# Cross attention on one core: GpSimd's work laid out turn by turn

## What is computed

```python
q = (x @ Wq + bq).reshape(b, ql, H, D_Q)          # b=16, ql=100, H=16, D_Q=64
k = (ctx @ Wk + bk).reshape(b, kl, H, D_Q)        # kl=1444
v = (ctx @ Wv + bv).reshape(b, kl, H, D_Q)
scores = einsum('bqhd,bkhd->bhqk', q, k) / sqrt(D_Q)
attn = softmax(scores, axis=-1)
out = einsum('bhqk,bkhd->bqhd', attn, v).reshape(b, ql, H * D_Q) @ Wo + bo
y = layernorm(x + out) * gamma + beta
```

## Time and profile before

| | us |
|---|---|
| median of 3 runs | 888.61 (886.81 to 889.89) |
| the profiled execution | 888.62, span 886.8 |
| TensorE busy | 860.3 (97%) |
| VectorE busy | 832.9 (94%) |
| ScalarE busy | 732.0 (83%) |
| GpSimd busy | 483.2 (54%) |

### The profile page before, as it was taken

How to read it: one execution, slowest core, us unless ns; L and a number is a source line. 1 busy time by engine, 2 the same in 40 slices (tenths; PEclk the granted TensorE clock), 3 DMA queues, 4 the chain that set the end, 5 groups by cost and what they waited for, 6 DMA issues and landing times.

```text
span 886.8 us, 19588 instructions
## 1 busy us (share of the span) xinstructions
PE 860.3 (97%) x7328; PEld 618.4 (70%) x7328; DVE 832.9 (94%) x1053; ACT 732.0 (83%) x989; POOL 483.2 (54%) x516
## 2 busy tenths in 40 slices
PE   8799999899999999999999999999999999999996
PEld 7476766577677677776777776766777777767675
DVE  4899899999999999999999999999999999998984
ACT  3687868888888888898988887888888988888983
POOL 2142497975637385465727555373854657276210
PEclk7999999999999999999999999999999999999999
DMA  9598988999999999999999999999999999999995
GB/s 238 130 165 192 192 164 171 209 206 191 227 194 225 216 218 218 220 216 219 213 206 231 211 197 222 196 219 227 214 217 214 216 221 217 194 205 209 210 180 125
DMA packets 683041, 180.79 MB, mean 204 GB/s; under 512 B 654596, under 2 KB 682052, under 8 KB 682948
## 3 DMA queue, kind: packets, MB, share of 16 engines
q1 hardware_dynamic: 681332, 178.48, 102.3%
q10 hardware_dynamic: 1344, 0.53, 0.2%
q0 software_dynamic: 272, 0.53, 0.2%
HBM read 15.35 MB, written 0.82 MB: 18 GB/s over the span
## 4 chain that ended last, share of the span: by engine, by line
DVE 43%; PE 38%; issue 8%; ACT 5%; DMA 5%; SPq 2%; ACTq 0%; DVEq 0%; POOLq 0%; POOL 0%
DVE p_lo L921 20%; PE ps L642 17%; DVE nmax L906 16%; PE ps L603 16%; DMA pt_hi<-p_hi 4%; ACT p L1030 2%; PE ps L458 2%; ACT p_hi L1038 2%; DVE rsum L912 2%; PE ps L450 1%; DVE rinv L914 1%; DVE c_max L808 1%; PE ps L465 1%; DMA bq_pairs<-in_L_xattn_bq_dram 1%; SPq L402 1%
## 5 line engine op out<-in xcount | busy, mean ns | idle before, releaser
L921 DVE SCALAR_TENSOR_TENSOR p_lo<-p,rinv,p_hi 128x1444 f16<-128x1444 f32 x200 | 367.9, 1840 | 2.4 <-ACT p_hi L1038 2.0
L1038 ACT ACTIVATE p_hi<-p,rinv 128x1444 f16<-128x1444 f32 x200 | 299.7, 1499 | 57.3 <-DVE rinv L914 53.4
L906 DVE TENSOR_REDUCE nmax<-ps 128x1 f32<-128x1446 f32 x200 | 330.0, 1650 | 6.0 <-PE ps L603 6.0
L1030 ACT ACTIVATE p<-ps,nmax 128x1446 f32<-128x1446 f32 x200 | 292.7, 1464 | 48.6 <-DVE nmax L906 45.7
L642 PE MATMUL ps<-pt_hi,c_hi 128*128 128x256 f16 (+1 forms) x1232 | 253.6, 261 | 5.4 <-DMA pt_hi<-p_hi 3.8
L642 PE MATMUL ps<-pt_hi,c_lo 128*128 128x256 f16 (+1 forms) x1232 | 253.4, 261 | 0.0
L603 PE MATMUL ps<-ct_hi,g_hi 128*128 128x482 f16 (+3 forms) x624 | 155.9, 368 | 0.7 <-ACT p L1030 0.6
L603 PE MATMUL ps<-ct_hi,g_lo 128*128 128x482 f16 (+3 forms) x624 | 156.2, 368 | 0.0
L603 PE MATMUL ps<-ct_lo,g_hi 128*128 128x482 f16 (+3 forms) x624 | 156.2, 368 | 0.0
L642 PEld LDWEIGHTS ps<-pt_hi,c_hi 128*128 128x128 f16 x1232 | 114.4, 98 | 43.0 <-issue 10.4
L1137 POOL CAST g_hi<-g_raw 128x400 f16<-128x400 f32 x60 | 32.5, 542 | 203.7 <-DVE g_raw L831 203.7
(11 more groups left out here) (128 smaller groups left out, 820.2 us busy)
## 6 DMA issues: line engine op xcount, KB each, us to landing
c_raw<-in_ctx_dram SPq DMA_DIRECT2D x32, 256.0 KB
pt_hi<-p_hi SPq DMA_TRANSPOSE x200, 3.5
pt_lo<-p_lo SPq DMA_TRANSPOSE x200, 3.6
c_raw<-in_ctx_dram SPq DMA_DIRECT2D x16, 192.0 KB
c_raw<-in_ctx_dram SPq DMA_DIRECT2D x48, 18.0 KB
out_dram<-late_sb SPq DMA_DIRECT2D x16, 50.0 KB
x_sb<-in_x_dram SPq DMA_DIRECT2D x1, 600.0 KB
o_t<-in_L_xattn_Wq_dram SPq DMA_DIRECT2D x2, 256.0 KB, 4.5
```

The lines of the kernel that those rows point to most:

```text
L906: dve.tensor_reduce(nmax[:, n % RING:n % RING + 1], ps[:, bank:bank + 3, 0:KEYW], AX.XY, ALU.max, negate=True).then_inc(s_nm, 1)
L921: dve.scalar_tensor_tensor(out=p_lo[:, n % LOS, 0:KL], in0=p32[:, n % P32S, 0:KL], scalar=rinv[:, i:i + 1], in1=p_hi[:, par, 0:KL], op0=AL ...
L1030: act.activation(p32[:, n % P32S, :].rearrange("p (k w) -> p k w", w=KEYW), ps[:, bank:bank + 3, 0:KEYW], ACT.Exp, bias=nmax[:, i:i + 1], ...
L1038: act.activation(p_hi[:, par, 0:KL], p32[:, n % P32S, 0:KL], ACT.Copy, scale=rinv[:, i:i + 1]).then_inc(s_hi, 1)
```

## The change

GpSimd's program becomes one loop over turns. At the head of turn n it waits until VectorE has written the low part of tile n-1 (s_lo). Then come the pieces of that turn: the scales of the next queries and a result split at r = 0, a result split at r = 1, a query split at each of r = 2 to 5, a context piece at each of r = 6, 8 and 9 (CLO_AT), the last result split at r = 7, the tail copies, the inverse deviation and the first result split of the current batch at r = 10, finish_rows at r = 11. The once-only pieces get turns of their own: the matrices' low parts n = 13 to 16, the addition to x n = 18, x's low parts n = 19 to 22, M's low parts n = 24 to 27. These use a scratch tile of their own, left_scaled. SyncE's transpose ct_lo moves to r = 10 in every window.

```diff
-    CT_LO_AT = 8
-    CT_LO_AT_FIRST = 9
+    CT_LO_AT = 10
+    CLO_AT = (6, 8, 9)
...
+        left_scaled = sb("left_scaled", [P, HG * P])
...
-                if r == (CT_LO_AT if w else CT_LO_AT_FIRST) and w + 1 < B:
+                if r == CT_LO_AT and w + 1 < B:
                     transpose_context_lo(w + 1)
...
-            def context_lo(b):
-                par = b % 2
+            def context_lo(b, g):
+                par, tiles = b % 2, slice(TG * g, TG * g + TG)
                 pool.wait_ge(s_al, b + 1)
...
-            for w in range(B):
-                b = w + 1
...
+            def once(n):
+                g = n - A16_AT - 1
+                if 0 <= g < NG:
+                    pool.wait_ge(s_16h, g + 1)
+                    heads = slice(HG * g, HG * g + HG)
+                    leave_lo(g, a_sb[:, heads, :], a16[:, heads], ax_scale[:, 0:1])
+                if n == X16_AT:
...
+                    pool.tensor_tensor(x_sb[:, :, :], x_sb[:, :, :], rows_b[0:QL, 0:1, :].to_broadcast([QL, B, D]),
+                                       ALU.add).then_inc(s_xres, 1)
+                g = n - X16_AT - 1
+                if 0 <= g < NX:
...
+                g = n - M16_AT - 1
+                if 0 <= g < NG:
+                    leave_m_lo(g)
+
+            for n in range(N):
+                w, r = window(n)
+                b, g_at = w + 1, (G_AT if w else G_AT_FIRST) + 1
+                if n > 0:
+                    pool.wait_ge(s_lo, n)
+                if b < B and r == (0 if w else g_at - 1):
+                    query_scales(b)
+                if in_parts(w - 1) and r < 2:
+                    if w == 2 and r == 0:
+                        pool.wait_ge(s_16, NG + NX)
+                        split_results(w - 1, 0)
+                    split_results(w - 1, r + 1)
+                if b < B and g_at <= r < g_at + NG:
+                    split_queries(b, r - g_at)
+                once(n)
+                if b < B and r in CLO_AT:
+                    context_lo(b, CLO_AT.index(r))
+                if in_parts(w - 1) and r == 7:
                     split_results(w - 1, NG - 1)
                     output_scale(w - 1)
...
+                if r == 10:
+                    if b < B:
+                        pool.wait_ge(s_cl, NT * b)
+                        context_tail(b)
+                    if w > 0:
+                        inverse_deviation(w - 1)
+                    if w > 1 and in_parts(w):
+                        split_results(w, 0)
+                if r == 11 and w > 0:
                     finish_rows(pool, w - 1)
             inverse_deviation(B - 1)
```

More of the change, by code:

```diff
@@ L1158, in leave_m_lo @@
             def leave_m_lo(g):
-                heads, at = slice(HG * g, HG * g + HG), c_scaled[:, :].rearrange("p (n w) -> p n w", w=P)
+                heads, at = slice(HG * g, HG * g + HG), left_scaled[:, :].rearrange("p (n w) -> p n w", w=P)
                 pool.wait_ge(s_mh, g + 1)
@@ L1162, in leave_m_lo @@
                     pool.wait_ge(s_ml, g)
+                else:
+                    pool.wait_ge(s_16, NG + NX)
                 pool.tensor_scalar(at, m_sb[:, heads, :], m_scale[:, :], 1.0, ALU.mult, ALU.mult).then_inc(s_mw, 1)
@@ L1173, in context_tail @@
                 pool.tensor_copy(c_tail[0:2 * KTAIL, par, :], c_hi[0:2 * KTAIL, par, KT - 1, :]).then_inc(s_chl, 1)
-            def context_lo(b):
-                par = b % 2
+            def context_lo(b, g):
+                par, tiles = b % 2, slice(TG * g, TG * g + TG)
                 pool.wait_ge(s_al, b + 1)
[L1178 to L1189, removed]
+                if NT * b + g > NT:
+                    pool.wait_ge(s_cl, NT * (b - 1) + g)
+                pool.tensor_scalar(c_scaled[:, :], c_raw[:, par, tiles, :].rearrange("p t d -> p (t d)"),
+                                   alpha[:, par:par + 1], 1.0, ALU.mult, ALU.mult).then_inc(s_cs, 1)
+                pool.wait_ge(s_cs, NT * (b - 1) + g + 1)
+                pool.wait_ge(s_chi, NT * b + g + 1)
+                pool.tensor_tensor(c_lo[:, par, tiles, :].rearrange("p t d -> p (t d)"), c_scaled[:, :],
+                                   c_hi[:, par, tiles, :].rearrange("p t d -> p (t d)"), ALU.subtract).then_inc(s_cl, 1)
             def inverse_deviation(b):
@@ L1199, in leave_lo @@
                 n, w = raw.shape[1], raw.shape[2]
-                at = c_scaled[:, 0:n * w].rearrange("p (n w) -> p n w", w=w)
+                at = left_scaled[:, 0:n * w].rearrange("p (n w) -> p n w", w=w)
                 if i:
@@ L1217, in _ @@
                              bv_sb[:, :].unsqueeze(2).to_broadcast([P, PAIRS, P])).then_inc(s_bvw, 1)
-            for w in range(B):
-                b = w + 1
-                if b < B:
-                    query_scales(b)
[L1223 to L1234, removed]
+            def once(n):
[5 more added lines that the diff above has]
+                if n == X16_AT:
+                    emptied(pool, J_R)
+                    emptied(pool, J_X3)
+                    pool.wait_ge(s_ax, 2 * NG)
+                    pool.tensor_tensor(x_sb[:, :, :], x_sb[:, :, :], rows_b[0:QL, 0:1, :].to_broadcast([QL, B, D]),
+                                       ALU.add).then_inc(s_xres, 1)
+                g = n - X16_AT - 1
+                if 0 <= g < NX:
+                    pool.wait_ge(s_16h, NG + g + 1)
+                    batches = slice(XG * g, XG * g + XG)
+                    leave_lo(NG + g, xT[:, batches, :], x16[:, batches], ax_scale[:, 1:2])
+                g = n - M16_AT - 1
+                if 0 <= g < NG:
+                    leave_m_lo(g)
@@ L1235, in _ @@
                     split_results(w - 1, NG - 1)
                     output_scale(w - 1)
[L1237 to L1255, removed]
@@ L1256, in _ @@
-                if w > 0:
-                    inverse_deviation(w - 1)
+                if r == 10:
[7 more added lines that the diff above has]
+                if r == 11 and w > 0:
                     finish_rows(pool, w - 1)
```

## The result

| | us |
|---|---|
| before, median | 889.25 (886.81 to 890.25, 4 runs) |
| changed kernel, median | 927.98 (925.42 to 932.22, 4 runs) |
| ratio after/before | 1.0439, 95% interval 1.0415 to 1.0463 |
| profiled execution, span | 930.3 |

What follows compares the result with a forecast made beforehand. TensorE was taken to bound the kernel. Onto 888.6 us came even-window stalls 24.9, window 0 1.8, odd windows 0.7 and clock 7, less 3 at the start: 920.0 us, range 905 to 932.

Steps and rivals of the forecast that it cites:

- The deciding term: Late ct_lo transpose stalls TensorE in the shared tile's scores, ends of windows 2 to 14: 7 x 3.55 = 24.9 us.
- VectorE's lag: From the end of a tile's scores to VectorE's start on them; taken as 0.35 us in each even-window stall.
- Odd windows: With 13 tiles, ct_lo lands just in time: 0 to 0.4 us each, taken as 0.1, seven times: 0.7 us.
- Window 0: ct_lo moves from r = 9 to 10 and lands late: between 0 and 2.6 us, taken as 1.8.
- The clock: TensorE's granted clock falls to 0.50 behind stalls: 1.4 us in five of seven, 7 us, bounds 0 and 12.
- The start: TensorE's early waits for first output rows and M's low parts shrink: gain 0 to 5.2 us, taken as 3.
- VectorE's low part: Line 921, held up by GpSimd in the kernel before; its mean should fall from 1.84 to 1.74 us or less.
- The overrun at r = 10: GpSimd's pieces exceed the gap between low parts: nothing to 0.95 us, taken as 0.5 us a window.
- the relief: VectorE's low parts freed from GpSimd: per two windows 1.8 us given back of 2.4, worth zero on the path.
- context_scale's new wait of 0.4 us: At r = 10 VectorE's context_scale waits for tail copies started that turn: nothing to two casts of 0.52 us.
- TensorE bounds, with VectorE 2% behind: Over 25 turns, tiles 87 to 112, TensorE is busy 102.86 of 102.86 us and VectorE has 1.8 us free.

Runs made afterwards that it cites:

- the filler experiment: Changed kernel with 17 extra matmuls, 3.5 us in all, before the wait for ct_lo at the ends of even windows 2 to 14: 917.58 us, ratio 1.0324.
- the kernel with r = 9: Changed kernel with ct_lo issued one turn earlier, CT_LO_AT = 9, GpSimd still turn by turn: 888.66 us, ratio 0.9997 to the kernel before.
- the load: Extra VectorE memset of 256 columns every turn: 924.75 us in the kernel before, 900.76 us in GpSimd turn by turn with ct_lo at r = 9.
- the new order with less work for TensorE: GpSimd turn by turn, ct_lo at r = 9, without the products of c_lo with pt_hi: 880.12 us, ratio 0.9896 to the kernel before.

## Why the prediction held, and where it was off

- **The deciding term was right in mechanism and place.** Queue order, two tiles of lead in even windows, a stall before the new batch's products of the third part: the traces show each, and one number put back by one removes the loss. Its size was short: 7 x 3.55 = 24.9 us forecast, 29.0 measured, and the gap came in seven places, not eight. What was mis-sized is VectorE's lag. I took 0.35 us, on the argument that VectorE catches up when TensorE is held. At tile 85 it is 410.40 - 409.67 = 0.73 us, and 0.73 to 1.60 in the seven even windows, 6.9 us in sum where I had 2.5. Right before that row maximum stand the rows of the last batch (take_rows, their last instruction at 410.30), which I had left out. The 2.93 us that a pt_lo held the queue at one tile add some 1.4, and the product that waits is the second of the third part, 0.2 us after the one I counted to, which takes 1.4 off. The end of p_hi came 5.14 us after the row maximum's start, as forecast; from ct_lo's issue to the waiting product it took 3.45 to 3.83 us, where I had 3.6.
- **Odd windows:** 0.7 forecast, 3.4 measured, by the same lag: 0.88 us or more instead of 0.35 turns "just in time" into 0.1 to 1.0 us.
- **Window 0:** 1.8 forecast, none measured. TensorE stood 1.87 us for ScalarE before (as in the earlier trace rows, 1.82), this time with a fall of the clock behind it, and came to the third part at 82.45, when ct_lo had just landed.
- **The clock:** 7 us forecast, about 10 by the filler experiment. I counted five falls of 1.4 us; there were seven, two of them twice as long. How many there are isn't fixed by the stall: the kernel before with the late transpose had six for stalls as long. (In the trace of the kernel before, the clock was at 0.50 in two more stretches than the earlier trace rows name, 10.24 us from 11 us on and the last 2 us.)
- **The start:** -3 forecast. In the kernel with r = 9 tile 37's row maximum comes 3.5 us earlier than before (195.8 against 199.3 us), and TensorE no longer waits for M's low parts or the first output rows. That agrees.
- **VectorE's low part:** a mean of 1.74 or less was named, 1.79 measured. The overrun at r = 10 is as forecast (2.37 instead of 1.71 us), but the first 37 tiles, with several pieces in one turn, still hold 7 us of surplus. The 1.74 also didn't follow from my own terms: 0.5 us of overrun in each of 16 windows is a mean of 1.755.
- **context_scale's new wait of 0.4 us** doesn't exist: it waits for the tail copies of the window before, not for those of its own turn. I misread the count by one. Off the path, it cost nothing.
- **"TensorE bounds, with VectorE 2% behind"** was wrong in the second half. The 1.8 us that the earlier trace rows leave VectorE are handovers; without a third of the weighing 25 turns still take 102.6. The conclusion that the relief is worth nothing in time survives (0.9997 with it), but by 0.2 us in 25 turns, not 1.8. The stretch of the earlier trace rows was also one of the quiet ones: from tile 112 to 137 25 turns took 105.2 us, with TensorE idle for 2.

The sum, by measured terms: 29.0 + 3.4 of stalls, about 10 of clock and -3.5 at the start are 38.9 us, against 927.98 - 889.25 = 38.7. That it fits so closely is luck: the stalls are read from the profiled execution, which at 932.22 us is the slowest of the four, 43.6 us over the profiled one before, and there the same terms leave 14.7 us for the clock. The forecast of 920.0 is 8 us short: even and odd stalls and the clock were taken 9.8 us too low together, and window 0, taken 1.8 us too high, hid a part of that.

## What to carry to other kernels

A step that is moved in a queue must be placed by its landing, not by its issue: add up what stands before it in that queue, its own time in the queue and its flight, and compare with the first reader in the shortest window, here 12 turns and not 13. Two turns of lead looked ample and were 3.7 to 5.0 us too few. Add the lag of the engine that writes the source as well: one turn earlier was enough in the full kernel, and too late again by up to 1.8 us once VectorE lagged by up to 3. And relief on an engine that doesn't end the turns last is cover: it brought nothing here, and 24.0 us as soon as that engine was loaded.

## What the runs showed that was not expected

Idle time in a timeline isn't free time. VectorE keeps 1.33 us idle in 25 turns even under the load. And the recorded duration of a small instruction is not its cost on the engine. A memset recorded at 165 ns did move the row maximum right behind it, from 0.08 to 0.22 us after the inverse's start (the expectation of the wider one, which says under 0.05, has this wrong); but a turn without another job became only 0.09 us longer in the median, and turns with a job hardly at all, which is the 0.03 us a turn above. One recorded at 272 ns (256 columns) brought 25 turns in the new order to 105.25 us, against 102.03 over the same tiles in the new order with less work for TensorE: 0.13 us each. Useless matmuls of 3.6 us in front of each of seven waits made the kernel 10 us faster in all, as the granted clock then stayed at 1.00.
